# Fills of 16-bit products behind the products for maxima in an attention and expert kernel

## The chip, the cores and the metric

The kernel runs on one core of one Trainium2 chip. The metric is the device time of one execution in microseconds, as the median of several runs. The engines of a core are TensorE (PE in the rows; PEld is its weight load), VectorE (DVE), ScalarE (ACT), GpSimd (POOL) and the DMA queues of SyncE (SP). TensorE's clock has two levels, 1.2 and 2.4 GHz; the profile gives the granted share of the higher one, so 0.50 is half clock and 1.00 full clock.

## What is computed

The input is 2048 tokens of 256 features. Four blocks follow each other, each with a layer norm in front and a residual sum behind: attention a (layer 0), experts, attention b (layer 1), experts again. Cut to what matters here:

```python
# attention, 16 heads of 16 features, causal
q, k, v = ...                                     # projections of the normed tokens
scores = einsum('bhqd,bhkd->bhqk', q, k)          # plus a slope per head times (j - i) in layer 0
scores = where(j <= i, scores, -inf) / sqrt(D)
ctx = einsum('bhqk,bhkd->bqhd', softmax(scores), v)
x = x + ctx @ Wo + bo
# experts: 8 of 64 for each token, and a shared one
topv, topi = top_k(x @ gate_w.T, 8)
out = sum over the chosen e of softmax(topv)[e] * (silu(gate_e) * up_e) @ dp_e
```

The softmax subtracts each row's maximum, so every score is needed twice: once for the maximum, once for the exponential.

## The kernel before, in words

In attention the queries go in four blocks `b` of 512 (`QB`) and the heads in four groups `g` of four; `BLOCKS` lists the sixteen pairs, the last group with its blocks from last to first. For each pair TensorE makes two passes over the scores.

The first pass is for the maxima. One item `("max", g, b, k)` is a product of up to 512 columns that has the queries in rows, into one of three rotating banks (`max_banks`, `NMAX` = 3), and VectorE reduces it to one maximum a row (L2139; L2145 for the items in several pieces). The operands are 32-bit, and a head's features with its slope terms take 50 rows (48 in layer 1) in one half of the array's 128; `hh` is the half, and neighbouring items take turns. On the diagonal the product has one or two pieces (`parts`), and behind each piece two 16-bit products (L1685) add the causal mask. When a block's maxima are reduced, VectorE takes the minimum of their negatives, TensorE turns it (`"turn"`, L1693), VectorE splits it in a high and a low part, and DMAs on SP's queue (L995) write it into rows of `Qp`, so that the second pass subtracts it.

The second pass has the keys in rows. An item `("qk", ...)` is two products into one of two score banks (`exp_banks`, L1707), `"pv"` multiplies the exponentials that ScalarE wrote with the values (L1721), and `"ctx"` turns the finished sums (L1733).

`core_plan` puts these items in one list with a planner that knows costs and due times. TensorE, VectorE, ScalarE and GpSimd each go through that list in order and do their part of each item. While a block's minima are on their way there are only maxima of the next block left to do, and at the end of a block only its last maxima, so the list has runs of maxima without scores or sums. Each layer has seven of them with at least six items, and both layers use the same list. They start at about 59, 92, 122, 163, 269, 371 and 422 us in layer 0 and at 1029, 1060, 1089, 1133, 1238, 1340 and 1391 us in layer 1; below they are the first to the seventh run. A wait for a free bank stands in front of every item for maxima (`max_bank`), and one for the exponentials of the scores but one before (`exp_done`) in front of the scores.

Of the kernel before, what the change touches and what calls it, by code (L numbers as in the profile page):

```python
# [17 lines left out]
P = 128  # L18
# [79 lines left out]
             ("project", 3)])  # L98
EARLY_STEPS = (10, 14, 16, 17, 19, 20, 26, 30, 32, 33, 35, 36, 61, 62)
EARLY_NORM = 40  # L100
SCALE_BEHIND, DIVIDE_BEHIND = 3, 20
AHEAD = 2
WARM = {0: 5, 2: 10, 3: 2}
# [205 lines left out]
    return plan  # L309


def down_set(n):

    return 0 if n < SINGLE else n % NBUF


def down_before(n):

    return max(k for k in range(n) if down_set(k) == down_set(n))
# [131 lines left out]


def build(nc, A, parts="afbf"):
    plan = core_plan()
    tensor_plan, scalar_plan, vector_plan = expert_plan()
    ctx = ExitStack()
    with ctx:
        def sem(name):
            return ctx.enter_context(nc.semaphore(name))

        def tile(name, shape, dt=F32, stack=ctx):
            return stack.enter_context(nc.sbuf_tensor(f"{name}_t", shape, dt))


        exp_banks = [ctx.enter_context(nc.psum_tensor(f"exp_banks{i}", [P, 2, QB], F32)) for i in range(2)]
# [16 lines left out]
        ident16 = tile("ident16", [P, 2, P], BF16)  # L482
# [46 lines left out]
        fill = tile("fill", [S // FILL, FILL], F32R, pre)  # L529
# [121 lines left out]
        exp_done = sem("exp_done")  # L651
# [74 lines left out]
        for i, kind in enumerate(parts):  # L726
            n = parts[:i].count("f") if kind == "f" else "ab".index(kind)
# [35 lines left out]
        n = 0  # L763
# [9 lines left out]
        SQ = len(sq_of)  # L773
# [36 lines left out]
        def block_no(layer, g, b):  # L810
            return layer * G * NB + BLOCKS.index((g, b))
# [13 lines left out]
        def down_bank(n, side):  # L825
            return BANK[down_set(n) * 2 + side][:, 0:PW]

        def down_banks(n):
            return exp_banks[down_set(n)][:, :, 0:PW]
# [703 lines left out]
        def _(pe):  # L1533
# [108 lines left out]
            def attention(kind, layer):  # L1642
# [10 lines left out]
                wait_all_freed(pe, core_unit[layer])  # L1653
                pe.wait_ge(ident_ready, 10)
                pe.wait_ge(values_set, 2 * layer + 2)
                begun = set()

                def before(s):
                    return sum(FRESH_LOADS[i] + (s + 1) * LOADS[i] for i in range(layer))
# [1 line left out]
                for item in plan:  # L1661
                    if item[0] == "max":
                        _, g, b, number = item
# [12 lines left out]
                        for p, r, c in parts:  # L1676
# [4 lines left out]
                            if c == b:  # L1681

                                rows = slice(hh * HALF, (hh + 1) * HALF)
                                for a in range(2):
                                    last = pe.matmul(bank[:, end - P + a * HALF:end], ident16[rows, a, :],  # L1685
                                                     cut16[rows, a, a * HALF:P], start=False, stop=a == 1)
                        last.then_inc(max_product, 1)
                    elif item[0] == "turn":
                        _, g, b = item
                        n = block_no(layer, g, b)  # L1690
# [4 lines left out]
                    elif item[0] == "qk":  # L1695
                        _, g, b, j, p, _ = item
# [5 lines left out]
                        sq = layer * SQ + sq_of[item]  # L1702
# [7 lines left out]
                    elif item[0] == "pv":  # L1710
                        _, g, b, j, _ = item
                        e = e_of[layer, g, b, j]
                        off = P * max(0, j - TPB * b)
                        n = block_no(layer, g, b)
# [5 lines left out]
                        for h in range(GH):  # L1720
                            last = pe.matmul(pv_banks[n % NPV][32 * h:32 * h + 32, off:QB],  # L1721
                                             values[:, j, GH * g + h, :], probs[:, e % NP, h, off:QB],
                                             start=(j == 0), stop=(j == TPB * (b + 1) - 1))
                        last.then_inc(pv_done, 1)
                    elif item[0] == "ctx":
                        _, g, b = item
                        n = block_no(layer, g, b)
# [9 lines left out]
                    elif item[0] == "turn_ctx":  # L1737
                        _, b, k = item
# [20 lines left out]
            for kind, n in phases:  # L1759
                if kind != "f":  # L1760
                    attention(kind, n)
                else:
                    experts_pe(pe, n, turn, router)


        def experts_dve(dve, f, statistics, normalise, projection):
# [211 lines left out]
            for kind, n in vector_plan:  # L1978
# [45 lines left out]
                elif kind == "combine":  # L2024
# [15 lines left out]
                    if n % (TPB * TOPK) == TPB * TOPK - 1:  # L2040
                        dve.wait_ge(combined, f * 2 * NG + n + 1)
                        statistics(phase, t // TPB)
                    if n == NG + EARLY_NORM:
                        normalise(phase, MIDDLE[2])
# [241 lines left out]
```

## Time and profile before

| | |
|---|---|
| median of 3 runs | 1961.71 us (1954.36 to 1966.47) |
| profiled execution, its own time | 1967.3 us |
| span in the profile | 1965.5 us |
| mean granted clock of TensorE | 0.889 |
| TensorE busy | 1680.7 us, 86% of the span |
| VectorE busy | 1428.1 us, 73% |
| ScalarE busy | 1127.5 us, 57% |
| GpSimd busy | 695.3 us, 35% |

The page cuts the span into 40 slices of 49 us. A table of stretches gives each engine's busy time in a stretch, with the number of its instructions in brackets, then the mean granted clock, the DMA share and GB/s. The timeline gives start and length of a group of like instructions, and in square brackets how long the engine was idle before and for whom it waited. Matmuls overlap in the array, and their ends are modelled, so a busy TensorE is not one at its peak: the distance between two starts says more than a length.

### The profile page before, as it was taken

To read this page: it belongs to the slowest core of one execution; us is meant where nothing else is said; L and a number is where in the kernel's file an instruction comes from. 1 tells how busy PE (TensorE), PEld (TensorE's weight loads), DVE (VectorE), ACT (ScalarE), POOL (GpSimd) and SP (SyncE) were. 2 spreads that over 40 slices of the span, in tenths; PEclk is the share of its full clock that TensorE was granted. 3 is DMA by queue.
4 is the path that set the end of the run, shared out by engine and by line. 5 is a ranking of instruction groups with operands and counts; after the bars stand their busy time and mean duration, and the time that the engine had idled before them with its cause. 6 is when DMAs were issued, how large, how long until landed. Compare 5 with 4: busy or idle time off the path is not lost.

```text
span 1965.5 us, 36378 instructions
## 1 busy us (share of the span) xinstructions
PE 1680.7 (86%) x12410; PEld 1039.2 (53%) x12410; DVE 1428.1 (73%) x3057; ACT 1127.5 (57%) x1999; POOL 695.3 (35%) x788
## 2 busy tenths in 40 slices
PE   6899999999978799987788999999999777889910
PEld 5545444445556677774334454544446566777710
DVE  5678888888577865885547788888865787558843
ACT  2145767577557677764233558585674676776710
POOL 6000101000257556445660001010012674754466
PEclk9678989899979999998895789898998898999965
DMA  6540120300065656665752204031002555666643
GB/s 233 173 70 2 24 45 13 56 2 2 31 265 165 182 172 199 207 198 184 239 188 50 32 2 64 4 49 18 2 7 101 217 175 166 204 189 201 203 146 118
DMA packets 127906, 225.96 MB, mean 115 GB/s; under 512 B 15364, under 2 KB 91028, under 8 KB 123444
## 3 DMA queue, kind: packets, MB, share of 16 engines
q1 hardware_dynamic: 103152, 156.49, 26.4%
q0 software_dynamic: 24576, 67.14, 12.5%
q8 instruction: 106, 1.74, 0.4%
q14 instruction: 72, 0.59, 0.1%
HBM read 124.20 MB, written 98.84 MB: 113 GB/s over the span
## 4 chain that ended last, share of the span: by engine, by line
PE 57%; DVE 12%; DMA 11%; issue 7%; POOL 7%; ACT 3%; SPq 1%; ACTq 0%; DVEq 0%; POOLq 0%
PE late_banks L1721 14%; PE late_banks L1679 12%; PE exp_banks L1707 8%; PE late_banks L1510 6%; PE exp_banks L1527 6%; POOL ring_t L1086 4%; DMA ring_t<-token_rows,index_t 4%; DMA ring_t<-expert_rows,rows_of_t 3%; DVE inter_t L2020 3%; POOL ring_t L1081 2%; DVE chunk_max_t L2139 2%; DMA expert_rows<-outs_t 2%; PE late_banks L1485 2%; PE late_banks L1685 2%; PE late_banks L1543 2%
## 5 line engine op out<-in xcount | busy, mean ns | idle before, releaser
L1339 ACT ACTIVATE probs_t<-exp_banks 128x1024 f32<-128x1024 f32 (+3 forms) x640 | 539.2, 896 | 294.6 <-PE exp_banks L1707 292.0
L2139 DVE TENSOR_REDUCE chunk_max_t<-late_banks 128x1 f32<-128x512 f32 (+1 forms) x960 | 603.0, 682 | 115.8 <-PE late_banks L1679 89.6
L1177 POOL TENSOR_SCALAR_AFFINE_SELECT probs_t<-probs_t 128x512 f32<-128x512 f32 x128 | 81.2, 635 | 681.5 <-ACT probs_t L1339 681.5
L1721 PE MATMUL late_banks<-probs_t,values_t 128*32 128x512 f32 (+3 forms) x2560 | 320.0, 575 | 1.9 <-POOL probs_t L1177 1.1
L1086 POOL DMA_INDIRECT ring_t<-expert_rows,rows_of_t x256 | 243.7, 952 | 188.9 <-DVE x_sb_t L2038 126.6
L1510 PE MATMUL late_banks<-tokensT_t,fetched_t 128*128 x2048 | 297.5, 290 | 11.5 <-ACT fetched_t L1243 5.1
L1081 POOL DMA_INDIRECT ring_t<-token_rows,index_t x256 | 248.7, 972 | 140.5 <-PE late_banks L1485 83.4
L2020 DVE TENSOR_TENSOR inter_t<-late_banks,silu_t 64x256 f32<-64x256 f32 x512 | 217.5, 425 | 89.1 <-ACT silu_t L1260 78.2
L1510 PEld LDWEIGHTS late_banks<-tokensT_t,fetched_t 128*128 128x128 f32 x2048 | 254.1, 195 | 41.9 <-issue 23.0
L1679 PE MATMUL late_banks<-contextT_t,Qp_t 50*128 50x512 f32 (+7 forms) x640 | 234.4, 515 | 9.6 <-DVE chunk_max_t L2139 2.2
L1527 PE MATMUL exp_banks<-fetched_t,inter_t 64*128 64x128 f32 x2048 | 187.6, 303 | 45.8 <-DVE inter_t L2020 43.7
L1679 PE MATMUL late_banks<-Kp_t,Qp_t 50*128 50x512 f32 (+7 forms) x640 | 211.5, 464 | 3.7 <-DVE chunk_max_t L2139 2.1
L1243 ACT ACTIVATE fetched_t<-weights_t 128x384 f32 x320 | 159.1, 519 | 72.7 <-PE exp_banks L1527 60.0
L2038 DVE SCALAR_TENSOR_TENSOR x_sb_t<-ring_t,row_top_t,x_sb_t 128x256 f32<-128x256 f32 x256 | 122.9, 480 | 97.8 <-DMA ring_t<-expert_rows,rows_of_t 93.8
L1527 PEld LDWEIGHTS exp_banks<-fetched_t,inter_t 64*128 64x128 f32 x2048 | 137.9, 191 | 89.4 <-DVE inter_t L2020 68.4
L1679 PEld LDWEIGHTS late_banks<-contextT_t,Qp_t 50*128 50x128 f32 (+1 forms) x640 | 115.0, 221 | 132.0 <-DVE chunk_max_t L2139 103.2
L1266 ACT ACTIVATE outs_t<-exp_banks 128x512 f32<-128x512 f32 x256 | 150.5, 588 | 41.6 <-PE exp_banks L1527 26.6
L1679 PEld LDWEIGHTS late_banks<-Kp_t,Qp_t 50*128 50x128 f32 (+1 forms) x640 | 101.5, 200 | 131.3 <-DVE chunk_max_t L2139 102.7
L1707 PE MATMUL exp_banks<-Qp_t,contextT_t 52*128 52x512 f32 (+7 forms) x640 | 149.7, 442 | 14.4 <-DMA Qp_t<-neg_lo_t 10.3
L1707 PE MATMUL exp_banks<-Qp_t,Kp_t 52*128 52x512 f32 (+7 forms) x640 | 141.6, 421 | 7.5 <-ACT probs_t L1339 5.3
L2010 DVE COPY fetched_t<-weights_t 128x384 f32 x192 | 82.8, 431 | 62.2 <-PE exp_banks L1527 58.0
L1485 PE MATMUL late_banks<-ident_t,ring_t 128*128 128x128 f32 x512 | 98.8, 290 | 32.2 <-DMA ring_t<-token_rows,index_t 27.7
(228 smaller groups left out, 1886.4 us busy)
## 6 DMA issues: line engine op xcount, KB each, us to landing
expert_rows<-outs_t SPq DMA_DIRECT2D x256, 256.0 KB
weights_t<-in_experts SPq DMA_DIRECT2D x8, 1728.0 KB, 13.8
Qp_t<-q_rows SPq DMA_DIRECT2D x12, 768.0 KB
weights_t<-in_experts SPq DMA_DIRECT2D x4, 2112.0 KB, 10.4
q_rows<-part_hi_t SPq DMA_DIRECT2D x16, 512.0 KB, 3.9
k_rows<-part_hi_t SPq DMA_DIRECT2D x16, 512.0 KB, 4.5
Kp_t<-k_rows SPq DMA_DIRECT2D x8, 768.0 KB
q_rows<-part_lo_t SPq DMA_DIRECT2D x16, 256.0 KB, 5.1
```

What stands on the lines that cost most here:

```text
L1081: pool.indirect_dma_start(ring[:, slot, :], None, token_rows[f][:, :], bass.IndirectOffsetOnAxis(ap=index[h][:, n:n + 1], axis=0))\
L1086: pool.indirect_dma_start(ring[:, slot, :], None, expert_rows[f][h][:, :], bass.IndirectOffsetOnAxis(ap=rows_of[:, t, k:k + 1], axis=0))\
L1243: act.activation(fetched[:, n % NFETCH, blk, :], weights[:, bass.ds(fetches[n][blk], EW)], ACT.Copy)\
L1266: act.activation(outs[:, out % NOUT, :, :].rearrange("p b (s c) -> p s b c", s=2), down_banks(n).rearrange("p s (b c) -> p s b c", b=2), A ...
L1339: act.activation(probs[:, e % NP, 2 * p:2 * p + 2, off:QB], exp_banks[sq % 2][:, :, off:QB], ACT.Exp, scale=D ** -0.5).then_inc(exp_done, 1)
L1510: last = pe.matmul(bank[:, blk * P:(blk + 1) * P], fetched[:, n % NFETCH, blk, k * P:(k + 1) * P], tokensT[:, bass.ds(starts_of[n][blk] + ...
L1527: last = pe.matmul(down_bank(n, side)[:, blk * P:(blk + 1) * P], inter[rows, n % 2, blk * P:(blk + 1) * P], fetched[rows, n % NFETCH, blk, ...
L1679: last = pe.matmul(bank[:, begin:end], Qp[s][rows, p, t * P:(t + 1) * P], Kp[s][rows, p, c * QB:c * QB + end - begin], start=True, stop=c < b)
L1707: last = pe.matmul(exp_banks[sq % 2][:, hh, off:QB], Kp[s][rows, p, j * P:(j + 1) * P], Qp[s][rows, p, b * QB + off:(b + 1) * QB], start=T ...
L1721: last = pe.matmul(pv_banks[n % NPV][32 * h:32 * h + 32, off:QB], values[:, j, GH * g + h, :], probs[:, e % NP, h, off:QB], start=(j == 0) ...
L2020: dve.tensor_tensor(inter[side * EI:(side + 1) * EI, n % 2, :], up, silu[0:EI, n % 2, :], ALU.mult)\
L2139: op = dve.tensor_reduce(chunk_max[:, b, p, chunk_row(r), chunk_col(b, r, c)], bank[:, 0:n].rearrange("q (p k) -> q p k", p=len(parts)), A ...
```

## The change

`with_fills` goes through the finished list and inserts items. Where a run of items without scores and sums holds at least six for maxima (`FILL_RUN`), each of these is followed by an item `("fill", scored)`, but for the last one of the run and those right ahead of a turn. TensorE does a fill as two products (`FILLS`) of the 16-bit identity on all 128 rows with 384 columns (twice the 192 of `FILL_COLS`) into the score bank that the next scores will overwrite. The values written there are read by nobody. In front of the first fill for a given pair of scores stands the same wait for the exponentials as in front of the scores. The other engines have no part in a fill. There are 92 in the list, so 184 in the program, with 368 products: 33 of a list's fills stand behind plain products of 512 columns, 26 behind diagonal products of the last row of tiles, which have one piece and two masks, and 33 behind diagonal products in two pieces with four masks.

```diff
+FILLS, FILL_COLS = 2, 3 * P // 2
+FILL_RUN = 6
...
+def with_fills(plan):
+
+    filled, run, scored = [], [], 0
+
+    def close(run):
+        fills = sum(item[0] == "max" for item in run) >= FILL_RUN
+        for n, item in enumerate(run):
+            filled.append(item)
+            if fills and item[0] == "max" and n + 1 < len(run) and run[n + 1][0] != "turn" and \
+                    any(later[0] == "max" for later in run[n + 1:]):
+                filled.append(("fill", scored))
+
+    for item in plan:
+        if item[0] in ("max", "turn", "ctx", "out", "scale", "divide"):
+            run.append(item)
+            continue
+        close(run)
+        run = []
+        filled.append(item)
+        scored += item[0] == "qk"
+    close(run)
+    return filled
...
 def build(nc, A, parts="afbf"):
-    plan = core_plan()
+    plan = with_fills(core_plan())
...
+                    elif item[0] == "fill":
+                        sq = layer * SQ + item[1]
+                        if sq >= 2 and sq not in begun_fills:
+                            pe.wait_ge(exp_done, sq - 1)
+                        begun_fills.add(sq)
+                        twice = ident16[:, :, :].rearrange("p a c -> p (a c)")[:, 0:FILL_COLS]\
+                            .rearrange("p (o c) -> p o c", o=1).broadcast_to([P, 2, FILL_COLS])
+                        for _ in range(FILLS):
+                            pe.matmul(exp_banks[sq % 2][:, 0, 0:2 * FILL_COLS].rearrange("p (o c) -> p o c", o=2),
+                                      ident16[:, 0, :], twice, start=True, stop=True)
```

The order of TensorE's instructions shows it at two places. The first is in the third run, behind the transposes of the context: diagonal products in two pieces (128 and 384 columns) with their masks. Before:

```order
L1733 MATMUL late_banks<-ident_t,sums_t 128x128 x4
L1679 MATMUL late_banks<-contextT_t,Qp_t 128x128
L1685 MATMUL late_banks<-cut_t,ident_t 128x128
L1685 MATMUL late_banks<-cut_t,ident_t 128x64
L1679 MATMUL late_banks<-contextT_t,Qp_t 128x384
L1685 MATMUL late_banks<-cut_t,ident_t 128x128
L1685 MATMUL late_banks<-cut_t,ident_t 128x64
L1679 MATMUL late_banks<-contextT_t,Qp_t 128x128
```

The changed kernel at the same place (its lines are 26 to 36 further down):

```order
L1769 MATMUL late_banks<-ident_t,sums_t 128x128 x4
L1705 MATMUL late_banks<-contextT_t,Qp_t 128x128
L1711 MATMUL late_banks<-cut_t,ident_t 128x128
L1711 MATMUL late_banks<-cut_t,ident_t 128x64
L1705 MATMUL late_banks<-contextT_t,Qp_t 128x384
L1711 MATMUL late_banks<-cut_t,ident_t 128x128
L1711 MATMUL late_banks<-cut_t,ident_t 128x64
L1722 MATMUL exp_banks<-ident_t 128x384 x2
L1705 MATMUL late_banks<-contextT_t,Qp_t 128x128
```

Two more products of 384 columns now stand between one such item and the next. The second place is the end of the same run, around the turn (L1693, in the changed kernel L1729) up to the first scores (L1707). Before:

```order
L1685 MATMUL late_banks<-cut_t,ident_t 128x64
L1679 MATMUL late_banks<-contextT_t,Qp_t 128x512 x2
L1693 MATMUL late_banks<-ident_t,neg_max_t 16x128
L1679 MATMUL late_banks<-contextT_t,Qp_t 128x512 x6
L1707 MATMUL exp_banks<-Qp_t,contextT_t 128x512 x4
```

And in the changed kernel, up to the third product behind the turn:

```order
L1711 MATMUL late_banks<-cut_t,ident_t 128x64
L1722 MATMUL exp_banks<-ident_t 128x384 x2
L1705 MATMUL late_banks<-contextT_t,Qp_t 128x512
L1722 MATMUL exp_banks<-ident_t 128x384 x2
L1705 MATMUL late_banks<-contextT_t,Qp_t 128x512
L1729 MATMUL late_banks<-ident_t,neg_max_t 16x128
L1705 MATMUL late_banks<-contextT_t,Qp_t 128x512
L1722 MATMUL exp_banks<-ident_t 128x384 x2
L1705 MATMUL late_banks<-contextT_t,Qp_t 128x512
L1722 MATMUL exp_banks<-ident_t 128x384 x2
L1705 MATMUL late_banks<-contextT_t,Qp_t 128x512
```

The order of the items for maxima, the turn and the scores is the same; five of the six products behind the turn have a fill behind them.

## Rows read from the trace of the kernel before

**Rows 1.** The page: TensorE's busy time, and its granted clock in 40 slices.
```profile
PE 1680.7 (86%) x12410; PEld 1039.2 (53%) x12410; DVE 1428.1 (73%) x3057; ACT 1127.5 (57%) x1999; POOL 695.3 (35%) x788
...
PEclk9678989899979999998895789898998898999965
```

**Rows 2.** Stretches from run to turn, layer 0: engines' busy us, clock, DMA share, GB/s.
```profile
59.20:66.90 7.70, 7.25 (x50) 4.74 (x51) 6.58 (x12) 0.00 (x0) 0.00 (x0) 0.67 1.03 324
92.50:97.20 4.70, 4.33 (x22) 2.53 (x19) 3.27 (x7) 0.99 (x2) 0.00 (x0) 0.50 0.00 0
122.10:129.35 7.25, 7.06 (x53) 4.36 (x49) 6.76 (x14) 0.99 (x2) 0.62 (x1) 0.81 0.51 87
163.30:173.55 10.25, 9.95 (x71) 6.93 (x67) 9.83 (x18) 0.99 (x2) 0.62 (x1) 0.71 0.00 0
268.90:275.20 6.30, 5.85 (x50) 4.16 (x46) 5.91 (x12) 0.99 (x2) 0.62 (x1) 0.86 0.01 3
370.60:376.65 6.05, 5.18 (x41) 3.00 (x37) 5.63 (x12) 0.99 (x2) 0.62 (x1) 0.93 0.01 3
...
1029.10:1037.80 8.70, 6.99 (x50) 4.62 (x51) 6.42 (x11) 0.00 (x0) 0.00 (x0) 0.62 0.78 201
```

**Rows 3.** Stretches of 4 us from the third run's start.
```profile
124.00:128.00 4.00, 4.00 (x31) 2.42 (x28) 3.69 (x8) 0.22 (x1) 0.62 (x1) 0.83 0.35 57
128.00:132.00 4.00, 3.68 (x9) 1.62 (x7) 3.93 (x9) 0.00 (x0) 0.00 (x0) 0.50 0.05 20
```

**Rows 4.** Stretches from first scores to the clock's rise; the sum of all fourteen.
```profile
76.90:92.50 15.60, 15.25 (x92) 8.23 (x92) 8.63 (x14) 5.20 (x8) 2.55 (x4) 0.50 0.00 1
...
1043.10:1060.10 17.00, 15.27 (x94) 8.03 (x94) 8.90 (x15) 6.48 (x9) 2.54 (x4) 0.50 0.00 1
...
sum 133.30, PE 128.71 PEld 59.30 DVE 75.81 ACT 70.07 POOL 5.09; mean PE 9.19 PEld 4.24 DVE 5.42 ACT 5.01 POOL 0.36
```

**Rows 5.** Timeline of TensorE in the third run and behind it.
```profile
123.72 0.32 PE L1679 MATMUL late_banks<-contextT_t,Qp_t 50*128 50x128 f32 x1
...
124.28 0.32 PE L1679 MATMUL late_banks<-contextT_t,Qp_t 50*128 50x128 f32 x1
...
125.28 0.50 PE L1679 MATMUL late_banks<-contextT_t,Qp_t 50*128 50x512 f32 x1
125.63 0.26 PE L1685 MATMUL late_banks<-cut_t,ident_t 64*128 64x128 bf16 x2
...
134.15 1.22 PE L1707 MATMUL exp_banks<-Qp_t,contextT_t 52*128 52x512 f32 x4 [0.62 <-DMA Qp_t<-neg_lo_t]
...
138.12 1.93 PE L1721 MATMUL late_banks<-probs_t,values_t 128*32 128x512 f32 x8
...
141.99 1.89 PE L1721 MATMUL late_banks<-probs_t,values_t 128*32 128x512 f32 x8
...
144.95 1.06 PE L1721 MATMUL late_banks<-probs_t,values_t 128*32 128x512 f32 x8
...
147.07 1.07 PE L1721 MATMUL late_banks<-probs_t,values_t 128*32 128x512 f32 x8
```

**Rows 6.** Timeline around the third run's turn: turn, reductions behind it, first exponentials.
```profile
129.35 0.37 PE L1693 MATMUL late_banks<-ident_t,neg_max_t 128*16 128x128 f32 x1 [0.19 <-DVE neg_max_t L2155]
...
130.82 3.66 DVE L2139 TENSOR_REDUCE chunk_max_t<-late_banks 128x1 f32<-128x512 f32 x6
...
134.98 3.87 ACT L1339 ACTIVATE probs_t<-exp_banks 128x1024 f32<-128x1024 f32 x4 [10.76 <-PE exp_banks L1707]
```

**Rows 7.** Timeline: the first scores of each layer, with the idle time before.
```profile
76.91 1.22 PE L1707 MATMUL exp_banks<-Qp_t,contextT_t 52*128 52x512 f32 x4 [5.81 <-DMA Qp_t<-neg_lo_t]
...
1043.13 1.22 PE L1707 MATMUL exp_banks<-Qp_t,contextT_t 50*128 50x512 f32 x4 [0.73 <-DMA Qp_t<-neg_lo_t]
```

**Rows 8.** Timeline: a weight load for maxima; eight full-row products of the experts.
```profile
123.72 0.18 PEld L1679 LDWEIGHTS late_banks<-contextT_t,Qp_t 50*128 50x128 f32 x1 [0.17 <-DVE chunk_max_t L2139]
...
800.28 1.16 PE L1510 MATMUL late_banks<-tokensT_t,fetched_t 128*128 x8
```

More of the change, by code:

```diff
@@ L1655, in attention @@
                 pe.wait_ge(values_set, 2 * layer + 2)
-                begun = set()
+                begun, begun_fills = set(), set()
                 def before(s):
```

## Prediction

> **What bounds the kernel now.** I began with the page: a span of 1965.5 us, TensorE busy for 86% of it, and the granted clock far from full in the first third and again in the middle [rows 1]. The two attention stages (about 59 to 470 us and 1029 to 1440 us) hold those stretches. So I laid the order of TensorE's work beside the timeline and cut each attention stage at its seven long runs of maxima (at least six products for maxima with neither scores nor sums between them; those are the places that the change fills). Two tables of stretches then tell the story.
>
> Inside a run [rows 2] the products for maxima are paced by VectorE: six reductions of 512 columns take 3.66 us, 0.61 us each [rows 6]. But the clock falls in every run that is entered at full clock: 4 us after the third run begins it goes through 0.83 to 0.50 [rows 3], though the matmul unit is recorded busy for 7.06 of 7.25 us there [rows 2]. In the run this matters little. What follows matters: the scores that start behind the run begin at half clock, and it stays half for 6 to 17 us. Over the fourteen stretches between the first scores and the clock's rise that is 133.3 us, with TensorE busy for 128.7 of them and VectorE for only 75.8 [rows 4]. Here TensorE is what ends last. One round of scores, sums and three maxima takes 3.87 us at half clock (sums starting at 138.12 and 141.99) and 2.12 us at full clock (144.95 and 147.07) [rows 5].
>
> Between the turned maxima of a block and its first scores stands a chain that no clock shortens: turn at 129.35, scores at 134.15, 4.80 us, ending in the wait for the rows of minima that come back by DMA [rows 5, 6]. Six products for maxima lie under it.
>
> **The change part by part.** It adds 92 fills a layer, 184 in all, each of two 16-bit products of 384 columns: 368 matmuls and their weight loads. Nothing is removed and no other item is moved. The wait in front of a fill (the exponentials of the last scores but one) costs nothing: the sums ahead of each run have already waited for those exponentials. The fill writes the score bank that the next scores overwrite, and it gives no signal, so VectorE, ScalarE and the DMA queues see nothing of it but time.
>
> *Price of a fill.* No 384-column 16-bit product stands in the trace. A 512-column product for maxima lasts 0.50 us and a 128-column one 0.32 us at full clock [rows 5], so 384 more columns cost 0.18 us, a fill 0.36 us, and at half clock twice that, 0.72 us. The lower bound is nothing, where VectorE is awaited anyway; the upper is these plus exposed weight loads (below).
>
> *Pitch of a product with its fill.* A plain 512-column product needs 0.35 us from its weights to the next instruction (125.28 to 125.63 [rows 5]), of which about 0.1 are weights that can load while the fill runs, so 0.25 + 0.36 = 0.61 us: VectorE's own pace, free. A last-row diagonal product with its two masks ends 0.13 us later: 0.72 us, 0.1 over. A diagonal product in two pieces with four masks takes 0.56 to 0.6 us (123.72 to the next at 124.28 [rows 5]): about 0.87 us with the fill, over VectorE by 0.25. Of the 92 fills of a layer 33 stand behind plain products, 26 behind last-row diagonals and 33 behind the two-piece ones.
>
> *Cost of each run up to its turn*, at full clock, against its row in [rows 2] (transposes of a context 0.6, no fill ahead of the turn). Third run: 5 x 0.87 + 4 x 0.72 + 2 x 0.61 + 0.6 - 0.36 = 8.7, against 7.25: +1.4. By the same count the first +1.2, fourth +1.6, fifth +1.2, sixth +0.9; the seventh has one fill ahead of its turn, +0.4. Behind the turn, four products of the fourth and fifth runs are two-piece, and with fills they take 5.0 us under a chain of 4.8: +0.7 for both. Elsewhere 5 x 0.61 + 0.35 = 3.4 us hide under it. The second run is entered at half clock: 4.3 us if it were at full clock, 8.6 if at half all through, against 4.70; I take the middle, +1.8. That is 9.2 us in the first layer. In the second layer it is 7.4, because its first run took 8.70 us with waits that cover the fills (1.0 less), and its second run may be entered at full clock (0.8 less). Together **16.6 us lost**.
>
> *Gain.* If the fills hold the clock, the scores behind a run start at full clock. The twelve stretches that are not the first block's sum to 133.3 - 15.6 - 17.0 = 100.7 us [rows 4]. At full clock they shrink by 1 - 2.12/3.87 = 0.45: 45.5 us. From that comes off the start, which the exponentials set: four at 0.97 us [rows 6], so the first sums can't come before 2.7 us, where the ratio would give 2.2 of 3.97: 0.5 x 12 = 6. That leaves 39.5 us. The first block's stretches (15.6 and 17.0 us of narrow products) are doubtful. In the first layer TensorE sits idle for 5.81 us ahead of them and in the second for 0.73 [rows 7], so I take nothing for the first and half of 0.45 x 17 for the second: 3.9. **43.4 us gained.**
>
> Sum: 43.4 - 16.6 = 26.8 us. The profiled execution's own time was 1967.3 us, so 1940.5; it lies 5.6 us over the median of the three runs (1961.71). A measurement is a median of such runs, so I give 1961.7 - 27 = **1935 us**. A stall that goes turns into VectorE's pace: in a full-clock round of 2.12 us it needs three reductions, 1.83 us, so at most 0.3 us of a round is left to any further gain.
>
> **A rule against the price.** In [rows 8] a single load of 128 columns lasts 0.18 us, eight would be 1.44; but eight expert products of 128 columns on all rows, each with such a load in front, take 1.16 us together, 0.15 each. So a load runs under the product ahead of it, on the same rows, and my pitch stands. The Trainium skill says otherwise on one point (TensorE: Matmul & The Clock Gate, "Part 3: Packing small matmuls"): a weight load overlaps running matmuls only where it goes to other rows. By that rule the load behind a fill, which is on all rows, could never hide; this case's trace disagrees for full rows.
>
> **The rivals.**
> 1. *The loads don't hide.* Behind every fill a 32-bit load of 0.18 us [rows 8] is exposed, on all 184: some 33 us, which leaves 1961.7 - 27 + 33 = 1968, no change. For it speaks that no full-row 16-bit product is followed by a 32-bit half-row load in the trace; against it the same-row overlap of [rows 8]. Chance 0.12.
> 2. *The clock falls anyway*, in the runs or in the 0.6 us wait ahead of the scores. Only the cost stays: 1961.7 + 17 = 1979, slower by 0.9%. For it: the clock falls at 126 us with no idle stretch in front of it [rows 2, 3], so what it answers to isn't idleness as the timeline shows it. The skill's page named above ("HAM oscillation") has it fall after gaps without work; by that rule there would be nothing here for a fill to mend, and the trace disagrees, since it falls without one. Against the rival: the first expert stage, whose products take all rows [rows 8], stands at nines in the clock's row of the page from 700 us on [rows 1], and rounds with sums, whose products take all rows too, keep full clock [rows 5]. Chance 0.12.
> 3. *Slower: fills at half clock.* A run entered at half clock stays there, and in the others the clock falls 4 us in, as now. At half clock a product with its fill takes 1.2 us for plain and 1.7 for two-piece ones, against 0.6 to 0.73 now. About 120 of the 184 fills would stand there (an estimate from the clocks in [rows 2]): +0.75 each on the mean, 90 us, +9 for the rest, less 11 hidden in the waits ahead of the scores: 2050 us. It decides once more than some 70 fills run at half clock. Against it: such a run leaves TensorE not a moment without streaming, while runs at half clock now end in waits for VectorE. Chance 0.06.
> 4. *More than forecast*: both first blocks keep full clock too (15 us in all, 4 counted) and the fill costs half. 1961.7 - 27 - 11 - 8 = 1916. Chance 0.15.
>
> **How the numbers follow.** Forecast (15 to 38 us gained) 0.55, rivals 0.12, 0.12, 0.06, 0.15. The range goes from just under rival 4 to rival 1, which leaves out rivals 2 and 3: 1912 to 1967. About 1% (20 us) is what a measurement tells from no change. Faster by over 1%: rival 4 and four fifths of the forecast, 0.59. Within 1%: the rest of the forecast, rival 1 and most of rival 2, 0.31. Slower: 0.10.
>
> **What would show it.** The granted clock in the stretches of [rows 4] at 1.00 instead of 0.50 would show the gain's first step; sums every 2.1 us right behind the first scores the second; third run, entry to turn, 8.7 us instead of 7.25 the cost. Plain products with fills at 0.61 us deny rival 1, at 0.75 or more confirm it. First scores of the second layer's first block at full clock, and that clock kept to the second run, would show the half that I left out. I am wrong if the clock is still 0.50 behind the runs, or if the second and fourth runs lengthen by more than 3 us each.

## Result and profile after

The changed kernel takes 2016.14 us (median of four runs, 2001.34 to 2040.71) against 1960.99 us. The ratio is 1.0246, with a 95% interval of 1.0204 to 1.0289: slower by 2.5%, outside the range. The run of 2040.71 us counts as a slow one, so it stands in the median and the ratio leaves it out. The times of the changed kernel also spread over 39 us, those of before over 12, and they go with the mean granted clock: 0.928, 0.920, 0.917 and 0.903 from the shortest to the longest. The profiled execution took 2001.34 us.

The page of the changed kernel, to be read against [rows 1] (the header has the span):

```profile
span 1999.4 us, 37114 instructions
...
PEclk9999999999989999998875999899999888999965
```

The clock did what the fills were to do in layer 0: the first ten slices are all nines. Yet the kernel is longer. The two attention stages show where. First before, from the first product for maxima to the last item of the stage, layer 0 and layer 1 (columns as in [rows 2]):

```profile
59.17:528.00 468.83, 449.82 (x3259) 221.05 (x3260) 368.97 (x646) 286.02 (x356) 50.46 (x80) 0.87 0.18 34
...
1029.10:1500.30 471.20, 453.49 (x3258) 221.45 (x3259) 369.00 (x646) 287.21 (x357) 50.46 (x80) 0.87 0.16 26
```

And the changed kernel:

```profile
59.73:528.03 468.30, 457.24 (x3442) 216.76 (x3443) 374.46 (x646) 285.03 (x356) 50.56 (x80) 1.00 0.17 34
1030.65:1532.80 502.15, 492.14 (x3442) 229.06 (x3443) 375.39 (x646) 286.55 (x357) 50.56 (x80) 0.91 0.14 25
```

Layer 0 went from 468.83 to 468.30 us with the clock from 0.87 to 1.00; layer 1 got 31 us longer. The runs of the changed kernel up to their turns, to set against [rows 2]: the first, third and fourth of layer 0, and the first two of layer 1:

```profile
59.70:71.80 12.10, 12.07 (x73) 6.10 (x73) 7.78 (x12) 0.00 (x0) 0.00 (x0) 1.00 1.04 349
...
116.60:127.90 11.30, 11.30 (x73) 5.90 (x69) 7.90 (x14) 0.99 (x2) 0.62 (x1) 1.00 0.39 62
158.50:174.10 15.60, 15.60 (x100) 8.23 (x96) 10.86 (x18) 0.99 (x2) 0.62 (x1) 1.00 0.01 1
...
1030.70:1050.10 19.40, 19.40 (x73) 8.56 (x73) 7.87 (x12) 0.00 (x0) 0.00 (x0) 0.55 0.35 90
1075.10:1084.80 9.70, 9.70 (x33) 3.93 (x29) 4.17 (x8) 0.99 (x2) 0.36 (x1) 0.50 0.00 1
```

The third took 7.25 us before and takes 11.30, the fourth 10.25 and 15.60, at full clock and with VectorE busy for about 70% of the time. VectorE now waits for TensorE in front of most reductions, as here in the fourth run, so TensorE is what ends last in a run:

```profile
168.04 0.69 DVE L2181 TENSOR_REDUCE chunk_max_t<-late_banks 128x4 f32<-128x512 f32 x1 [0.45 <-PE late_banks L1711]
```

In layer 1 the first two runs go at half clock and take 19.40 and 9.70 us, where they took 8.70 and 4.70. The first run of layer 0 got 4.40 us longer up to its turn, but its first scores come 17.7 us behind its start in both kernels: the wait of 5.81 us in [rows 7] covers it.

The stretches from first scores to the next run, to set against [rows 4] (there only up to the clock's rise): behind the third run of layer 0, and behind the first and second of layer 1:

```profile
132.45:158.50 26.05, 25.03 (x184) 10.28 (x183) 23.13 (x38) 20.61 (x24) 2.54 (x4) 1.00 0.00 1
1057.75:1075.10 17.35, 15.65 (x94) 8.31 (x93) 9.36 (x16) 6.48 (x9) 2.55 (x4) 0.50 0.00 1
1092.50:1114.70 22.20, 21.75 (x129) 9.29 (x128) 15.77 (x27) 12.93 (x16) 2.54 (x4) 0.73 0.88 125
```

The stretch behind the third run took 29.2 us before (134.15 to the next run at 163.33) and now 26.05. Added up over both layers, from the starts of the same items in both traces, the runs from entry to first scores got 59.8 us longer (18.4 in layer 0, 41.4 in layer 1) and the stretches behind them 29.2 us shorter (18.8 and 10.4). That is +30.6 of the +33.9 us in the span.

What a fill costs stands in the timeline of TensorE in the third run of the changed kernel (L1705 product for maxima, L1711 masks, L1722 fill), at full clock:

```profile
120.47 0.33 PE L1705 MATMUL late_banks<-contextT_t,Qp_t 50*128 50x128 f32 x1
...
121.18 0.50 PE L1722 MATMUL exp_banks<-ident_t 128*128 128x384 bf16 x2
121.61 0.33 PE L1705 MATMUL late_banks<-contextT_t,Qp_t 50*128 50x128 f32 x1
...
122.76 0.50 PE L1705 MATMUL late_banks<-contextT_t,Qp_t 50*128 50x512 f32 x1
...
123.72 0.50 PE L1705 MATMUL late_banks<-contextT_t,Qp_t 50*128 50x512 f32 x1
...
128.10 0.50 PE L1705 MATMUL late_banks<-contextT_t,Qp_t 50*128 50x512 f32 x1
128.53 0.50 PE L1722 MATMUL exp_banks<-ident_t 128*128 128x384 bf16 x2
128.96 0.50 PE L1705 MATMUL late_banks<-contextT_t,Qp_t 50*128 50x512 f32 x1
```

A two-piece diagonal with its fill has a pitch of 1.14 us (120.47 to 121.61), a last-row diagonal 0.96 us (122.76 to 123.72) and a plain product 0.86 us (128.10 to 128.96). I had 0.87, 0.72 and 0.61: each short by about 0.25. At half clock, in layer 1, a plain product with its fill takes 1.47 us where I had 1.2:

```profile
1050.36 0.79 PE L1705 MATMUL late_banks<-contextT_t,Qp_t 48*128 48x512 f32 x1
...
1051.83 0.79 PE L1705 MATMUL late_banks<-contextT_t,Qp_t 48*128 48x512 f32 x1
```

### The profile page after: what moved, and what is told of

The parts are those of the page before. It is cut to its first block, busy times and chain, and to the rows that moved or that the text cites. A ratio compares the mean times of both kernels' runs of the same rounds, so it can differ in the third digit from the quotient of the medians.

```text
span 1999.4 us, 37114 instructions
## 1 busy us (share of the span) xinstructions
PE 1731.1 (87%) x12778; PEld 1046.1 (52%) x12778; DVE 1442.0 (72%) x3057; ACT 1126.1 (56%) x1999; POOL 697.1 (35%) x788
## 4 chain that ended last, share of the span: by engine, by line
PE 62%; DVE 10%; DMA 10%; issue 7%; POOL 7%; ACT 3%; ACTq 0%; DVEq 0%; SPq 0%; POOLq 0%
PE late_banks L1705 15%; PE late_banks L1757 13%; PE exp_banks L1743 7%; PE late_banks L1536 6%; PE exp_banks L1553 5%; PE exp_banks L1722 4%; POOL ring_t L1112 4%; DMA ring_t<-token_rows,index_t 4%; DMA expert_rows<-outs_t 3%; DVE inter_t L2056 3%; DMA ring_t<-expert_rows,rows_of_t 3%; POOL ring_t L1107 2%; PE late_banks L1711 2%; PE late_banks L1569 2%; PE late_banks L1511 2%
## 5 line engine op out<-in xcount | busy, mean ns | idle before, releaser
L2175 DVE TENSOR_REDUCE chunk_max_t<-late_banks 128x1 f32<-128x512 f32 (+1 forms) x960 | 610.6, 684 | 119.5 <-PE late_banks L1705 73.7
L1757 PE MATMUL late_banks<-probs_t,values_t 128*32 128x512 f32 (+3 forms) x2560 | 305.7, 551 | 1.9 <-POOL probs_t L1203 1.1
L1705 PE MATMUL late_banks<-contextT_t,Qp_t 50*128 50x512 f32 (+7 forms) x640 | 236.4, 466 | 4.5 <-DVE values_t L2144 2.1
L1705 PE MATMUL late_banks<-Kp_t,Qp_t 50*128 50x512 f32 (+7 forms) x640 | 206.3, 432 | 0.8 <-DVE chunk_max_t L2175 0.6
L1705 PEld LDWEIGHTS late_banks<-contextT_t,Qp_t 50*128 50x128 f32 (+1 forms) x640 | 107.5, 198 | 151.6 <-DVE chunk_max_t L2175 88.1
L1705 PEld LDWEIGHTS late_banks<-Kp_t,Qp_t 50*128 50x128 f32 (+1 forms) x640 | 95.5, 185 | 131.0 <-DVE chunk_max_t L2175 93.5
L1743 PE MATMUL exp_banks<-Qp_t,contextT_t 52*128 52x512 f32 (+7 forms) x640 | 139.5, 406 | 9.2 <-ACT probs_t L1365 8.5
L1711 PE MATMUL late_banks<-cut_t,ident_t 64*128 64x64 bf16 (+1 forms) x1024 | 124.7, 215 | 0.0
```

What stands on the lines that cost most here:

```text
L1705: last = pe.matmul(bank[:, begin:end], Qp[s][rows, p, t * P:(t + 1) * P], Kp[s][rows, p, c * QB:c * QB + end - begin], start=True, stop=c < b)
L1743: last = pe.matmul(exp_banks[sq % 2][:, hh, off:QB], Kp[s][rows, p, j * P:(j + 1) * P], Qp[s][rows, p, b * QB + off:(b + 1) * QB], start=T ...
L2175: op = dve.tensor_reduce(chunk_max[:, b, p, chunk_row(r), chunk_col(b, r, c)], bank[:, 0:n].rearrange("q (p k) -> q p k", p=len(parts)), A ...
```

## Experiments

All edits are made to the changed kernel. In the comparison with e1 to e4 every kernel took some 90 us longer (before stood at 2051.39 us), in the traces of e1 to e4 mostly in the expert stages; ratios carry over, microseconds don't.

**e1: each fill on both halves.** Theory A is that going from a product on half the rows to one on all rows and back has a price, for one because the loads aren't hidden. Theory B is that the number of instructions is what costs.

```diff
-                            pe.matmul(exp_banks[sq % 2][:, 0, 0:2 * FILL_COLS].rearrange(...),
-                                      ident16[:, 0, :], twice, start=True, stop=True)
+                            for hh in range(2):
+                                rows = slice(hh * HALF, (hh + 1) * HALF)
+                                pe.matmul(exp_banks[sq % 2][:, hh, 0:2 * FILL_COLS].rearrange(...),
+                                          ident16[rows, 0, :], twice[rows], start=True, stop=True)
```

> Each full-row product of a fill is replaced by two on 64 rows, one for each half of the array, into two banks of the same scores; columns and waits stay. Theory A (the weight loads between a product on all rows and one on half the rows don't hide, which makes a plain product with its fill 0.86 us where I counted 0.61): here every load goes to a half whose product has begun, so the pitch goes back to 0.61 to 0.70 us, the runs at full clock lose some 4 us less each in the worst places, and the kernel is 20 to 35 us faster than the changed one (+15 to +30 us over before instead of +48). Theory B (the fill is dear because of the number of instructions, each handed out one by one): twice the instructions, so the pitch is 0.86 us or more and the time that of the changed kernel or longer. Both expect the same clock as with full rows.

Measured: 0.9962 of before (0.9926 to 0.9998). Its third and fourth runs up to the turn, and the stretch behind the third run:

```profile
117.80:125.59 7.79, 7.32 (x93) 5.09 (x89) 6.74 (x14) 0.99 (x2) 0.62 (x1) 1.00 0.46 78
165.25:174.90 9.65, 9.52 (x127) 7.00 (x124) 9.43 (x18) 0.99 (x2) 0.62 (x1) 1.00 0.01 2
130.39:165.25 34.86, 33.91 (x181) 12.95 (x181) 22.70 (x37) 20.68 (x24) 2.54 (x4) 0.71 0.00 0
```

The runs are back at 7.79 us (before the change 7.25, with the change 11.30) and 9.65 us (10.25 and 15.60), at full clock, with twice the instructions of the fills. The weight loads differ too. In the changed kernel the fill's load is recorded 0.43 us behind the product's; in e1 the load for the other half is recorded 0.01 us behind it:

```profile
130.25 0.11 PEld L1722 LDWEIGHTS exp_banks<-ident_t 128*128 128x128 bf16 x2 [0.25 <-issue]
130.68 0.18 PEld L1705 LDWEIGHTS late_banks<-contextT_t,Qp_t 50*128 50x128 f32 x1 [0.32 <-DVE chunk_max_t L2175]
...
126.09 0.18 PEld L1705 LDWEIGHTS late_banks<-contextT_t,Qp_t 50*128 50x128 f32 x1 [0.45 <-DVE chunk_max_t L2177]
126.10 0.11 PEld L1724 LDWEIGHTS exp_banks<-ident_t 64*128 64x128 bf16 x2
```

(The first two rows are the changed kernel's, the others e1's. VectorE, named in the second, had freed that bank before; the reductions around it wait for TensorE.) Theory B falls, and theory A stands, with more gained than I expected. But the third row of the table of stretches is new: the stretch of scores behind the third run goes at 0.71 and takes 34.86 us. It does so in layer 1 too. Its start, on TensorE:

```profile
130.39 0.73 PE L1745 MATMUL exp_banks<-Qp_t,contextT_t 52*128 52x512 f32 x4 [0.92 <-DMA Qp_t<-neg_lo_t]
...
132.01 0.50 PE L1745 MATMUL exp_banks<-Qp_t,contextT_t 52*128 52x512 f32 x2 [0.64 <-ACT probs_t L1365]
...
132.92 0.79 PE L1745 MATMUL exp_banks<-Qp_t,contextT_t 52*128 52x512 f32 x2
```

TensorE waits 0.92 us for the minima and 0.64 us for the exponentials, and right behind that its products have the lengths of half clock (0.79 for 0.50).

**e2: fills on the half of the product ahead only.**

```diff
-                filled.append(("fill", scored))
+                filled.append(("fill", scored, item[3] % 2))
...
+                        rows = slice(item[2] * HALF, (item[2] + 1) * HALF)
-                            pe.matmul(exp_banks[sq % 2][:, 0, 0:2 * FILL_COLS].rearrange(...),
-                                      ident16[:, 0, :], twice, start=True, stop=True)
+                            pe.matmul(exp_banks[sq % 2][:, item[2], 0:2 * FILL_COLS].rearrange(...),
+                                      ident16[rows, 0, :], twice[rows], start=True, stop=True)
```

> The two products of a fill go only to the 64 rows on which the product for maxima ahead of them ran. Theory A: no change of rows between product and fill, and the next item's load goes to the other half, so the pitch is 0.61 us, paced by VectorE, and no run loses more than 1 us at full clock. Whether the clock is held tells whether it was the fills as such or their taking all rows: if held, layer 0 is 15 us faster than before and the whole -10 to -25 us; if not held, the clock falls in the runs as before the change, and the kernel costs what fills at half clock cost, +10 to +30 us. Theory B: pitch 0.86 us as with full rows.

Measured: 0.9984 (0.9949 to 1.0019). The third run up to its turn, and the 10 us behind that turn:

```profile
117.60:125.40 7.80, 7.08 (x64) 4.36 (x60) 6.87 (x13) 0.40 (x1) 0.62 (x1) 1.00 0.23 41
125.40:135.00 9.60, 8.78 (x37) 3.76 (x36) 7.47 (x14) 3.87 (x4) 0.00 (x0) 0.52 0.01 3
```

The run is short again (7.80 us) with as many 16-bit instructions as in the change, and each fill is followed by a 32-bit load: neither their number nor the change of type is the price, the rows are. The clock lasts to the turn and then falls, so the gain behind the run is small.

**e3: no fills in the first two runs of layer 1.**

```diff
+                    elif item[0] == "fill" and layer == 1 and item[1] <= 8:
+                        continue
```

> The changed kernel without the fills in the first two runs of layer 1 (26 of 184), in which the clock was at half in its profile. Those two runs took 13.1 and 7.8 us longer than before. If the loss there is the fills at half clock alone, the kernel is 18 to 24 us faster than the changed one (ratio to before about 1.013 instead of 1.025). If the fills had been about to raise the clock and help later, it is less than 10 us faster.

Measured: 1.006 (1.0026 to 1.0095); my 1.013 was too high. The first run up to its turn in layer 0, where the program is that of the change, and in layer 1; then layer 1's second:

```profile
59.26:77.87 18.61, 18.61 (x72) 8.15 (x72) 7.87 (x12) 0.00 (x0) 0.00 (x0) 0.58 0.88 273
1086.86:1095.28 8.42, 6.98 (x50) 4.59 (x50) 6.42 (x11) 0.00 (x0) 0.00 (x0) 0.67 0.77 208
...
1117.55:1122.25 4.70, 4.32 (x22) 2.55 (x19) 3.27 (x7) 1.00 (x2) 0.00 (x0) 0.50 0.00 2
```

Layer 1's two runs are at 8.42 and 4.70 us again, where the change had 19.40 and 9.70. So fills at half clock make up much of the loss. From 1.025 to 1.006 are some 37 us, more than the 20.8 us that the two runs had grown up to their scores; the two ratios come from different comparisons, and where the rest lies isn't shown. And the first row shows that the instructions alone don't set the clock in the first run: the same instructions as in the changed kernel took 18.61 us at 0.58 here and 12.10 us at 1.00 there. This fits the wide spread of the times, which goes with the clock.

**e4: one full-row product in a fill.**

```diff
-FILLS, FILL_COLS = 2, 3 * P // 2
+FILLS, FILL_COLS = 1, 3 * P // 2
```

> One product of 384 columns in a fill instead of two. Theory A: the second product costs only its columns, 0.16 us, and the 0.25 us for the change of rows stays, so a plain product with its fill has a pitch of 0.70 us at full clock, a last-row diagonal 0.80 us, a two-piece one 0.97 us. Theory B: half the instructions, so the pitch falls by half of the excess, also to about 0.70. The question is the clock: if it is held with one product, some 20 us faster than the changed kernel (about +25 over before); if not, about as slow as that one.

Measured: 1.0345 (1.0271 to 1.0418). The clock wasn't held. Its mean over most of layer 0's attention is below that of before (0.87 over the whole stage):

```profile
59.00:470.00 411.00, 408.18 (x2565) 189.55 (x2567) 313.17 (x525) 212.70 (x264) 37.79 (x60) 0.82 0.19 37
```

The price of the rows is paid and the clock isn't held in return. My optimistic branch missed, and the other one was too mild.

**e5: the change again**, with no edit, beside e6 and e7.

> The changed kernel once more, beside before and the others of this call, since in the last comparison the expert stages of every kernel took some 90 us longer than in the first profiles, so only ratios carry over. Expected: 1.015 to 1.03 of before. The kernel without the fills of layer 1's first two runs stood at 1.006; if fills at half clock are the dear ones, this one is 15 to 30 us over before, with a wide spread, and in its profile the time lost sits in runs whose clock is at half.

Measured: 1.0263 (1.021 to 1.0315), 2009 to 2054 us. In its profile layer 0's first run is at 0.56 and takes 19.1 us, and its attention stage 493.5 us, against 468.3 in the first profile.

**e6: both halves, and fills in the waits at the end of a run.**

```diff
+TAIL_FILLS = 2
...
+        if fills and run[-1][0] != "project":
+            filled.extend([("fill", scored)] * TAIL_FILLS)
+            ends.append(len(filled))
...
+    for end in ends[::-1]:
+        places = [n for n in range(end, len(filled)) if filled[n][0] == "max"]
+        block = next(item for item in filled[end:] if item[0] == "pv")[1:3]
+        filled.insert(places[1] + 1, ("fill_pv", *block))
...
+                    elif item[0] == "fill_pv":
+                        ...   two products on all rows into pv_banks, behind the wait for sums_out
```

> Fills on both halves as in the first experiment, and two further fills behind the last product for maxima of each run, where that kernel's TensorE waited 0.92 us for the rows of minima, and one fill of two full-row products into the bank of the sums behind the second product after the first scores, where it waited 0.64 us for the exponentials. Theory C (the clock fell at the start of the scores in the third run of both layers, for 20.5 us, because of these two waits): it stays at full there, some 9 us less in each layer, and the kernel is 15 to 30 us faster than before. Rival (the stretch falls to half clock whatever stands at its start): as with fills on both halves, 0.995 of before.

Measured: 0.9858 (0.981 to 0.9906), 1935.78 us against 1963.86. That is what theory C forecast, though the fills at the two waits came in together, so it isn't shown which of them counts. The attention stage of layer 0, the third run from turn to scores, the stretch behind it, and layer 1:

```profile
59.93:509.60 449.67, 431.94 (x3695) 215.87 (x3696) 367.50 (x646) 285.10 (x356) 50.56 (x80) 0.99 0.18 35
124.04:128.84 4.80, 4.32 (x35) 2.25 (x36) 4.77 (x10) 0.00 (x0) 0.00 (x0) 1.00 0.05 17
128.84:154.68 25.84, 25.27 (x183) 10.19 (x183) 22.53 (x37) 20.61 (x24) 2.54 (x4) 1.00 0.00 1
...
1013.34:1467.80 454.46, 439.30 (x3695) 220.05 (x3696) 368.15 (x646) 286.20 (x357) 50.56 (x80) 0.97 0.16 27
```

And on TensorE the two waits, now 0.25 and 0.21 us:

```profile
128.84 0.74 PE L1763 MATMUL exp_banks<-Qp_t,contextT_t 52*128 52x512 f32 x4 [0.25 <-DMA Qp_t<-neg_lo_t]
...
130.46 0.50 PE L1763 MATMUL exp_banks<-Qp_t,contextT_t 52*128 52x512 f32 x2 [0.21 <-ACT probs_t L1374]
```

The chain from turn to scores is still 4.80 us: the fills sit in its slack. The attention stages are 19.2 and 16.7 us shorter than before the change.

**e7: full-row fills of 32 columns.**

```diff
-FILLS, FILL_COLS = 2, 3 * P // 2
+FILLS, FILL_COLS = 2, 16
```

> The two full-row products of a fill cut from 384 to 32 columns; rows, loads, banks and waits stay. Theory A (a fixed cost of about 0.25 us for going to all rows and back, with loads that don't hide): the two-piece diagonals keep a pitch of 0.8 us against 0.6 before the change, and the fourth run takes 12 to 13 us to its turn where it took 10.2 before the change and 15.6 with the full fill. Rival (the cost is the columns alone): it takes 10.2 to 10.6 us. The clock should fall in the runs as before the change, since nearly nothing is streamed; if it is held, the loads or the rows and not the columns count.

A single run took 2018.34 us, 1.028 of before. The fourth run's first two products, still at full clock:

```profile
169.04 0.49 PE L1705 MATMUL late_banks<-contextT_t,Qp_t 50*128 50x512 f32 x1
169.47 0.21 PE L1722 MATMUL exp_banks<-ident_t 128*128 128x32 bf16 x2
169.61 0.50 PE L1705 MATMUL late_banks<-contextT_t,Qp_t 50*128 50x512 f32 x1
```

The pitch is 0.57 us with only 64 columns in the two products of the fill together. The full fill's pitch is 0.86, and the difference of 0.29 us is what 704 more columns take at 2.4 GHz. From the product's load to the fill it is 0.43 us, as with the full fill; to a mask on the same rows it was 0.35 [rows 5]. So the rows' price is apart from the columns. As a whole the run took 17.1 us and not 12 to 13, because the clock fell in it to a mean of 0.59: the expected time was for full clock.

**e8 and e9: e1 and e6 again**, on one chip with e10, no edit.

> Fills on both halves, as in the first experiment, beside before and the next two on one chip. Expected 0.990 to 1.000 of before, with the clock held in most runs but lost at the start of the scores of some, the third run above all. If it comes out as fast as the kernel with the tail fills (0.986), the tail fills brought nothing and the chips differed.

> Fills on both halves with the tail fills, once more. Expected 0.980 to 0.990 of before, and faster than the kernel without the tail fills by 10 to 25 us, with less than 40 us at half clock in the two attention stages.

Measured: 0.9972 (0.9936 to 1.0007) and 0.9809 (0.9736 to 0.9883), 1959.27 and 1931.05 us against 1965.91. The tail fills are worth 28 us. But in e8 the third run of layer 0 ends in the same two waits as in e1, 0.91 and 0.66 us, and the clock stays full behind them:

```profile
130.22 0.73 PE L1745 MATMUL exp_banks<-Qp_t,contextT_t 52*128 52x512 f32 x4 [0.91 <-DMA Qp_t<-neg_lo_t]
...
131.84 0.50 PE L1745 MATMUL exp_banks<-Qp_t,contextT_t 52*128 52x512 f32 x2 [0.66 <-ACT probs_t L1365]
...
130.22:156.30 26.08, 25.08 (x184) 10.23 (x184) 22.79 (x37) 20.74 (x25) 2.54 (x4) 1.00 0.00 1
```

So the waits put the clock at risk and don't decide it: behind the sixth run, after a wait of 0.91 us too, its mean over 9.2 us is 0.63.

**e10: the tail fills alone.**

```diff
-            if fills and item[0] == "max" and n + 1 < len(run) and run[n + 1][0] != "turn" and \
-                    any(later[0] == "max" for later in run[n + 1:]):
-                filled.append(("fill", scored))
```

> Only the tail fills: two on both halves behind the last product for maxima of each run and one in front of the exponentials' wait, none behind the other products for maxima. If what loses the clock are the waits at the end of a run, this holds it as well, at 0.985 of before. If the clock is lost inside the run, behind products that use one half at a time, it falls as before the change (4 us into each run) and the kernel is the same as before within 0.5%, 0.998 to 1.005, with about 110 us at half clock in each attention stage.

Measured: 0.998 (0.9945 to 1.0015). The third run, and from its turn to the scores:

```profile
121.16:128.39 7.23, 6.52 (x52) 4.03 (x49) 6.73 (x14) 0.99 (x2) 0.62 (x1) 0.99 0.39 69
128.39:133.19 4.80, 4.66 (x14) 2.42 (x15) 4.77 (x10) 0.00 (x0) 0.00 (x0) 0.50 0.03 9
```

The clock is gone before the tail fills come. Each kind of fill alone is worth at most 0.4% (0.996 to 0.998); both together bring 1.4 to 1.9%.

**e11: the tail fills with full-row fills.** The edit is e6's without that of e1.

> The tail fills of the fastest kernel, but every fill on all 128 rows again, as in the change. It tells what the two halves are worth once the clock is held at the runs' ends. At full clock the full-row fills made the seven runs of a layer some 18 us longer than before (12 to 15 us longer than fills on both halves), and where the first runs of a layer are at half clock 10 to 20 us more. Theory A expects 0.995 to 1.015 of before, against 0.981 to 0.986 with both halves. If the rows hardly mattered and the clock at the start of the scores was everything, it would be within 0.5% of the tail kernel, 0.98 to 0.99.

Measured: 1.0361 (1.0315 to 1.0406), worse than both theories allowed. Layer 0's first run up to its turn, the third from turn to scores, and the fourth up to its turn:

```profile
59.27:77.92 18.65, 18.64 (x72) 8.16 (x73) 7.87 (x12) 0.00 (x0) 0.00 (x0) 0.58 0.79 263
154.51:160.20 5.69, 5.69 (x22) 2.06 (x21) 5.04 (x9) 0.00 (x0) 0.00 (x0) 1.00 0.02 4
186.06:201.67 15.61, 15.61 (x99) 8.20 (x96) 10.86 (x18) 0.99 (x2) 0.62 (x1) 1.00 0.00 0
```

At full clock the fourth run is 15.61 us again, 5.96 us over e1 and e6, and the tail fills, which sit in slack with both halves, add 1.1 us here (5.69 us for the 4.56 of the changed kernel, 127.89 to 132.45), since the run had none left. I had counted them as free. Between e6 and e11 lies 5% of the kernel, with only the rows of the fills changed. Not all of it is their price at full clock: the first two runs of both layers went at half clock in e11 (a mean of 0.51 from 62 to 132 us and from 1072 to 1152 us), while in the profile of the changed kernel only layer 1's did.

## Why the prediction was wrong, step by step

*What bounds the kernel, and the gain.* Right in kind. Where the clock was held, the stretches behind the runs shrank: 18.8 us in layer 0, for which I had 19.8 (half of 39.5). Two sizes were off. In layer 0 the first block's stretch, for which I took nothing, gave 4.3 of the 18.8 us. In layer 1 I counted on the same gain as in layer 0, and half clock in the first two runs left 10.4 us. Of the 43.4 us forecast, 29.2 came.

*Price of a fill.* The columns were nearly right: 0.29 us for 704 of them, so 0.32 for 768, where I had 0.36.

*Pitch of a product with its fill.* **This is the step that failed**: "of which about 0.1 are weights that can load while the fill runs". They don't: the load is recorded only behind the fill (e1). Going to all rows and back costs another 0.15 us: 0.43 us from the product to the fill instead of 0.35, and 0.43 us from the fill to the next product for 0.32 us of columns, less the 0.04 us by which I had the columns too dear. At 0.86 us plain products lost their cover under VectorE's 0.61, 0.96 and 1.14 replaced 0.72 and 0.87, and layer 0's seven runs grew by 18.4 us for my 9.2. My own signs of it came out: plain products above 0.75 us, and the fourth run up by more than 3 us (10.25 to 15.60). I had taken [rows 8] for proof that a load hides under a product on the same rows. It shows this between products that all take 128 rows; products on half the rows ahead of or behind full-row ones it doesn't show. Fills split by halves take the cost away (e1, e11).

*The rule against the price.* The Trainium skill's rule (TensorE: Matmul & The Clock Gate, "Part 3: Packing small matmuls"), by which a load overlaps only where it goes to other rows, was the better guide between half-row products and full-row fills: in e1, and in e2 for the load behind each fill, loads could go to the other half, and the cost was gone. Between products that all take 128 rows [rows 8] still speak against it. How much of the 0.25 us is the load and how much something else in the change of rows isn't separated; the 0.43 us from a product to a fill, against 0.35 to a mask, puts 0.08 in front of the fill.

*Rival 1* had the mechanism at 0.12 and came out at 33 us, since it priced 0.18 and not 0.25 a fill and kept the clock held everywhere. *Rival 3* was half right: the first two runs of layer 1 went at half clock and grew by 20.8 us up to the first scores (13.1 and 7.8), while the others held but for the end of the fifth. I had allowed for it only by "the middle, +1.8" for the one run that I took to be entered at half clock (in layer 0, where it was then entered at full clock), and had argued that a TensorE that never pauses would come back to full clock. It was busy for 19.40 of 19.40 us and stayed at 0.55. Both together are the result: the rows' price everywhere (9.2 us over my count in layer 0, and part of the 41.4 us in layer 1, where I had 7.4), half clock in some runs, and less gain. *Rival 2* did show, in another form: the clock can fall in the waits ahead of the scores (e1). In the changed kernel the full-row fills had used up the wait for the minima; the one for the exponentials stood, and the clock was kept behind it in the third run:

```profile
134.25 0.50 PE L1743 MATMUL exp_banks<-Qp_t,contextT_t 52*128 52x512 f32 x2 [0.66 <-ACT probs_t L1365]
```

*Range.* I took each rival by itself, let the range end at rival 1 (0.12) and left rival 3 (0.06) outside. What came was the two together, and they add up.

*Left open.* Why the first run holds the clock in one execution and loses it in the next, with the same instructions (e3 against the change), why in the changed kernel it fell in layer 1's first run with fills in place and no wait inside the run, and why e1 lost it behind the third run in both layers, while e8, the same program, lost it behind other runs. With the tail fills it was held behind the second to sixth runs of both layers in both profiles (e6, e9); which of the two waits mattered wasn't tried. The changed kernel and e8 only say that the wait for the exponentials doesn't always cost the clock.

## What to carry to other kernels

Work put in only to hold TensorE's clock must be cheaper than the slack of the place where it stands, and its price is the distance between two starts, not its columns: between products on half the rows, fill with products on halves. Hold the clock over the whole stretch, up to and into the waits at its end, or it can be lost there and with it most of what the fills bring (0.996 and 0.997 without the tail fills, 0.986 and 0.981 with them). Price each such run for half clock too: there a plain product with its fill took 1.47 us instead of 0.86, and in layer 1's first two runs the clock didn't come back for it.

## What the runs showed of the hardware

- Going from a 32-bit product on 50 rows to 16-bit ones on 128 rows and back has a price apart from the columns at full clock: 0.43 us from the product to the fill, against 0.35 to a mask on the product's rows, and a pitch of 0.57 us with fill products of 32 columns (e7), 0.86 with 384. Pairs of products on 64 rows each don't pay it: a run of 15.60 us takes 9.65 (e1).
- TensorE recorded busy without a pause can stay at half clock: 19.40 of 19.40 us busy at 0.55, later 9.70 of 9.70 at 0.50. The Trainium skill's statement (TensorE: Matmul & The Clock Gate, "Part 1: The HAM clock gate") that activity releases the throttle isn't borne out by these rows, as far as recorded busy time is activity.
- The clock fell behind two short waits (0.92 and 0.64 us) in e1 and was kept behind the same two (0.91 and 0.66 us) in e8; with fills that cut them to 0.25 and 0.21 us it was kept in e6.
- The same instructions can run at either level: the first run of layer 0 took 12.10 us at 1.00 in one profile of the program (the change) and 18.61 us at 0.58 in another (e3, the same up to there).
